# Keys, values and attention output as three float32r passes instead of fp32 products

## The reference

```python
x = x + conv(groupnorm(x))                # 4 experts of 1x1 convolutions, gated per pixel
t = tokens(x)                             # (batch, 784, 96)
t = t + attn(layernorm(t))
t = t + ffn(layernorm(t))                 # weights as signs, activations quantized by groups of 6 images

def attn(x):                              # 12 heads of 8 channels
    q, k, v = split(x @ qkv_w + qkv_b);  q = q * 8 ** -0.5
    fk, fv = f(k), f(v)                   # f(t) = t + 1 if t >= 0 else exp(t)
    A = einsum('bhdn,bhne->bhde', fk, fv) * gauss
    out = einsum('bhnd,bhde->bhne', q, A - lambda_full * A)
    return out @ proj_w + proj_b
```

## Time and profile before

| what | value |
|---|---|
| median of 3 runs | 830.62 us (829.88 to 832.27) |
| span of the profiled execution, first to last instruction | 829.6 us |
| median less span | 1.0 us |
| PE busy | 769.0 us, 93% of the span, 4663 matmul records |
| PE weight loads | 510.4 us, 62% |
| DVE busy | 636.5 us, 77% |
| ACT busy | 476.7 us, 57% |
| POOL busy | 180.2 us, 22% |
| first and last start of a kv product | 93.4 and 651.2 us |

### The profile page before, as it was taken

One profiled execution on the slowest core, in us unless ns is written; L12 is line 12 of the kernel. 1 busy time (PEld: TensorE's weight loads), 2 busy tenths in 40 slices (PEclk: granted clock), 3 DMA queues, 4 the chain that ended last, 5 costly groups with the idle time before them and its releaser, 6 DMA issues.

```text
span 829.6 us, 15136 instructions
## 1 busy us (share of the span) xinstructions
PE 769.0 (93%) x4663; PEld 510.4 (62%) x4663; DVE 636.5 (77%) x1945; ACT 476.7 (57%) x684; POOL 180.2 (22%) x209
## 2 busy tenths in 40 slices
PE   6798899999999999999999999999999999999991
PEld 3465566667666667666666766666766555555540
DVE  3576377877888878788877778887778468999997
ACT  2554445545555554545554555554553499988981
POOL 1440222332223232223232223233222000000000
PEclk8899989999999999999999999999999999999996
DMA  9950011101101101111110101010100101463333
GB/s 217 207 138 16 16 30 30 46 29 29 44 29 29 44 29 29 44 29 29 42 31 29 43 30 29 29 43 29 30 28 15 32 28 53 147 179 113 119 117 116
DMA packets 20351, 48.62 MB, mean 59 GB/s; under 512 B 4937, under 2 KB 5223, under 8 KB 20327
## 3 DMA queue, kind: packets, MB, share of 16 engines
q1 hardware_dynamic: 19928, 47.72, 21.0%
q10 hardware_dynamic: 399, 0.60, 0.3%
HBM read 29.51 MB, written 18.67 MB: 58 GB/s over the span
## 4 chain that ended last, share of the span: by engine, by line
PE 68%; DVE 11%; ACT 8%; issue 7%; SPq 3%; POOL 2%; DMA 1%; ACTq 0%; DVEq 0%; POOLq 0%
PE slot L1010 15%; PE slot L994 9%; PE slot L1017 7%; PE slot L1020 6%; PE slot L1158 6%; PE slot L1055 5%; PE slot L1187 5%; PE slot L1218 4%; PE slot L1222 4%; PE slot L862 4%; DVE stage L1470 4%; ACT stage L759 3%; SPq L442 3%; ACT hT L752 2%; PE slot L926 1%
## 5 line engine op out<-in xcount | busy, mean ns | idle before, releaser
L1436 DVE TENSOR_SCALAR tok<-tok,ln_mv,ln_rs 112x96 f32<-112x96 f32 x434 | 109.2, 322 | 58.2 <-POOL ln_rs L603 58.2
L1010 PE MATMUL slot<-hT,w2s 128*96 128x392 f32 x384 | 135.5, 503 | 3.0 <-ACT hT L752 2.3
L759 ACT ACTIVATE stage<-slot,minus_one 112x768 f32<-112x768 f32 x64 | 52.6, 822 | 125.6 <-PE slot L1055 123.3
L752 ACT ACTIVATE hT<-slot,b1c,w_unit 128x784 f32<-128x784 f32 x96 | 93.1, 1006 | 23.0 <-PE slot L994 23.0
L1010 PEld LDWEIGHTS slot<-hT,w2s 128*96 128x96 f32 x384 | 60.6, 164 | 64.1 <-issue 54.4
L603 POOL TENSOR_TENSOR ln_rs<-ln_ve,pow_half 112x7 f32<-112x7 f32 x62 | 91.8, 1481 | 4.8
L1017 PE MATMUL slot<-big,W1b 99*128 (+1 forms) x360 | 90.3, 332 | 2.1 <-ACT hT L816 0.6
L1020 PE MATMUL slot<-big,W1b 96*128 (+1 forms) x360 | 89.8, 330 | 0.0
L816 ACT ACTIVATE hT<-slot,s 128x784 f32<-128x784 f32 x90 | 80.3, 926 | 6.6 <-DVE stage L1554 6.3
L1442 DVE TENSOR_REDUCE ymax<-slot 128x784 f32 (+1 forms) x90 | 81.1, 956 | 0.1
L600 POOL TENSOR_TENSOR ln_ve<-ln_mv,ln_eps 112x7 f32<-112x7 f32 x62 | 12.5, 202 | 316.2 <-DVE ln_mv L1430 316.2
(11 more groups left out here) (190 smaller groups left out, 1285.2 us busy)
## 6 DMA issues: line engine op xcount, KB each, us to landing
out<-t2T SPq DMA_DIRECT2D x56, 294.0 KB, 2.6
xs<-in_x SPq DMA_DIRECT2D x32, 294.0 KB, 2.8
big<-in_x SPq DMA_DIRECT2D x7, 1176.0 KB, 15.3
xs<-out SPq DMA_DIRECT2D x24, 294.0 KB, 3.3
big<-out SPq DMA_DIRECT2D x1, 1764.0 KB, 11.6
out<-big SPq DMA_DIRECT2D x6, 294.0 KB, 2.6
big<-in_x SPq DMA_DIRECT2D x2, 588.0 KB, 24.1
con<-shape_consts ACTq DMA_DIRECT2D x1, 445.5 KB, 6.3
```

What stands on the lines that cost most here:

```text
L752: nc.scalar.activation(hT[:, t, :].rearrange("p (a n) -> p a n", a=2), halves(t, P), ACT.Relu, scale=w1_unit[:, t:t + 1], bias=b1c[:, t:t ...
L1010: ins = mm(S[k][0:C, h, 0:HALF], w2s[:, v, t, :], hT[:, t, h * HALF:(h + 1) * HALF], start=t == 0, stop=t == TILES - 1, skip_group_check=True)
L1436: ins = V.tensor_scalar(dst[:, j, :], src[:, j, :], ln_mv[n][:, j, 0:1], ln_rs[n][:, j:j + 1], ALU.subtract, ALU.mult)
```

## The change

Keys, values and attention output are each computed in three passes over float32r parts: high x high, high x low, low x high, accumulated in PSUM. The high part is what the former fp32 copy wrote, now with type float32r; the low part is the fp32 value less the high part. ACT writes the high parts xh_hi and R_hi in place of xh1T and R, from the same PSUM and at the same places of its order. DVE gets two new subtractions in each step, each reading PSUM and the high part in SBUF: xh_lo (96x784) between the statistics of tok2 and its normalization, after a wait for the ACT copy, and R_lo (97x96) between the statistics of tok1 and the three maxima, after a wait for the ACT copy of R. PE's kv(0) waits for xh_lo_ready instead of xh1T_ready, and the attention's output for r_lo_ready instead of r_ready. In the setup DVE makes both parts of the weights (two more instructions and two waits on itself), and POOL fills one more row with a constant. Declarations of semaphores and unchanged lines are left out of the diff.

```diff
@@ -168,6 +169,8 @@
         qkvw = sb("qkvw", [C + 1, 3 * C])
+        kvw_hi = sb("kvw_hi", [C + 1, 2 * C], F32R)
+        kvw_lo = sb("kvw_lo", [C + 1, 2 * C], F32R)
...
@@ -248,13 +251,15 @@
-        xh1T = sb("xh1T", [C + 1, HW])
+        xh_hi = sb("xh_hi", [C + 1, HW], F32R)
+        xh_lo = sb("xh_lo", [C + 1, HW], F32R)
...
-        R = sb("R", [C + 1, C])
+        R_hi = sb("R_hi", [C + 1, C], F32R)
+        R_lo = sb("R_lo", [C + 1, C], F32R)
...
@@ -419,7 +427,7 @@
-        CONSTS_SET = (ones_ready, 10)
+        CONSTS_SET = (ones_ready, 11)
@@ -527,8 +535,9 @@
-            pool.wait_ge(ones_ready, CONSTS_SET[1] - 2)
-            nc.gpsimd.memset(xh1T[C:C + 1, :], 1.0).then_inc(ones_ready, 1)
+            pool.wait_ge(ones_ready, CONSTS_SET[1] - 3)
+            nc.gpsimd.memset(xh_hi[C:C + 1, :].bitcast(F32), 1.0).then_inc(ones_ready, 1)
+            nc.gpsimd.memset(xh_lo[C:C + 1, :].bitcast(F32), 0.0).then_inc(ones_ready, 1)
@@ -774,7 +783,7 @@
-                    nc.scalar.copy(*channels(xh1T[0:C, :], 0)).then_inc(xh1T_ready, 1)
+                    nc.scalar.copy(*channels(xh_hi[0:C, :], 0)).then_inc(xh1T_ready, 1)
@@ -792,7 +801,7 @@
-                    nc.scalar.copy(R[:, :], S[3][0:C + 1, 0, 0:C]).then_inc(r_ready, 1)
+                    nc.scalar.copy(R_hi[:, :], S[3][0:C + 1, 0, 0:C]).then_inc(r_ready, 1)
@@ -1034,6 +1043,7 @@
                 pe.wait_ge(projb_loaded, 16)
+                pe.wait_ge(kvw_ready, 1)
@@ -1052,8 +1062,10 @@
                 def kv(q, k, j0, n):
                     for j in range(n):
-                        ins = mm(chunks(k, n, 256, 2 * C)[:, j, :], xh1T[:, (j0 + j) * TOK:(j0 + j + 1) * TOK],
-                                 qkvw[:, C:3 * C], start=True, stop=True, skip_group_check=True)
+                        cols = slice((j0 + j) * TOK, (j0 + j + 1) * TOK)
+                        for p, (x_part, w) in enumerate(((xh_hi, kvw_hi), (xh_hi, kvw_lo), (xh_lo, kvw_hi))):
+                            ins = mm(chunks(k, n, 256, 2 * C)[:, j, :], x_part[:, cols], w[:, :],
+                                     start=p == 0, stop=p == 2, skip_group_check=True)
                     ins.then_inc(kv_ready, 1)
@@ -1119,7 +1131,7 @@
                 if attend:
-                    pe.wait_ge(xh1T_ready, i)
+                    pe.wait_ge(xh_lo_ready, i)
@@ -1182,10 +1194,11 @@
                 if attend:
-                    pe.wait_ge(r_ready, i)
-                    for h in range(2):
-                        ins = mm(S[3][0:C, h, 0:HALF], R[:, :], xh1T[:, h * HALF:(h + 1) * HALF],
-                                 start=True, stop=True, skip_group_check=True)
+                    pe.wait_ge(r_lo_ready, i)
+                    for p, (w, x_part) in enumerate(((R_hi, xh_hi), (R_hi, xh_lo), (R_lo, xh_hi))):
+                        for h in range(2):
+                            ins = mm(S[3][0:C, h, 0:HALF], w[:, :], x_part[:, h * HALF:(h + 1) * HALF],
+                                     start=p == 0, stop=p == 2, skip_group_check=True)
                     ins.then_inc(ao_ready, 1)
@@ -1351,7 +1364,9 @@
-            V.tensor_scalar(qkvw[C:C + 1, C:3 * C], qkvw[C:C + 1, C:3 * C], 1.0, None, ALU.add)
+            link(V.tensor_scalar(qkvw[C:C + 1, C:3 * C], qkvw[C:C + 1, C:3 * C], 1.0, None, ALU.add))
+            link(V.tensor_copy(kvw_hi[:, :], qkvw[:, C:3 * C]))
+            V.tensor_tensor(kvw_lo[:, :], qkvw[:, C:3 * C], kvw_hi[:, :].bitcast(F32), ALU.subtract).then_inc(kvw_ready, 1)
             bn_unit(3, pairs_compared)
@@ -1478,6 +1493,11 @@
                     stats(1, tok2, 2 * i - 1)
+                if attend:
+                    dve.wait_ge(xh1T_ready, i)
+                    V.tensor_tensor(tokenwise(xh_lo[0:C, :]),
+                                    flat(0)[0:C, 0:CHUNKS * P].rearrange("p (j t) -> p j t", t=P)[:, :, 0:TOK],
+                                    tokenwise(xh_hi[0:C, :].bitcast(F32)), ALU.subtract).then_inc(xh_lo_ready, 1)
                 if ffn:
                     apply(1, tok2, tok2, f, xh2_ready)
@@ -1520,6 +1541,10 @@
                     stats(0, tok1, 1 if isinstance(i, int) and i == 0 else 2 * i)
+                if attend:
+                    dve.wait_ge(r_ready, i)
+                    V.tensor_tensor(R_lo[:, :], S[3][0:C + 1, 0, 0:C], R_hi[:, :].bitcast(F32),
+                                    ALU.subtract).then_inc(r_lo_ready, 1)
                 if ffn:
                     for t in range(TILES):
                         absmax(f, t, t)
```

More of the change, by code:

```diff
@@ L13 @@
 BF16 = mybir.dt.bfloat16
+F32R = mybir.dt.float32r
 I32 = mybir.dt.int32
@@ L365, in build @@
         xh1T_ready = sem("xh1T_ready")
+        xh_lo_ready = sem("xh_lo_ready")
+        kvw_ready = sem("kvw_ready")
+        r_lo_ready = sem("r_lo_ready")
         kv_ready = sem("kv_ready")
```

## The result

The changed kernel takes 837.54 us (median of 4 runs, 836.03 to 840.66) beside 831.10 us for the kernel before (4 runs): ratio 1.0079, 95% interval 1.005 to 1.0107. The profiled execution took 837.06 us with a span of 835.3, 5.7 above the span of before.

What follows compares the result with a forecast made beforehand. PE and DVE were taken as co-critical. 29 steps at 0.215 us later give 6.2, the ends 1.4; the sum of 7.6 on the median 830.62 gives 838.2 us, range 820 to 882.

Steps and rivals of the forecast that it cites:

- R_lo's insertion: DVE, ahead of the three maxima: wait for R's copy plus the subtraction insert 0.56 us a step.
- The sum of a step: Steady step, mix to mix: t2 comes 0.25 us later, PE's transposes and mix 0.215 later in the mean.
- kv's gain: kv(0) on PE's path: falls from 1.32 to 1.01 us, so A comes 0.31 earlier.
- Price of a kv pass: PE's keys and values: each pass with its weight load takes 0.084 us, at least 0.081.
- idle time before A: PE before A: the other 0.24 us saved in kv, beyond kv(0)'s 0.31, becomes idle time.
- PE's slack to t2: PE's transposes after DVE's t2: slack 0 in one kind of step and 0.07 us in the other.
- The output: PE's attention output: six passes at 0.166 us, 1.00 against 1.32; starts late for R_lo, ends 0.34 earlier, waits for t2.
- xh_lo hidden: DVE before tok2's normalization: the 0.97 us subtraction lies under POOL's root with 0.3 to spare and costs nothing.
- The ends: Outside the steady loop: +0.7 us in the last step, +0.7 in the first image, setup nothing; 1.4 together.
- PE's busy time: Whole run: PE busy some 20 us less in all, named as a sign that the forecast is right.
- R_lo finds a gap: Rival, DVE from A to t2: room there, so R_lo doesn't delay t2 and the time is 822 us; chance 0.12.
- A pass at half or full price of fp32: Two rivals, PE's passes: half price gives 882 us, chance 0.06; full price 985 or 1050 us, chance 0.14.

Runs made afterwards that it cites:

- output_only: Changed kernel with keys and values as fp32 products over xh_hi alone, attention output still in three passes; 844.57 us, ratio 1.0155.
- r_lo_after_max: Changed kernel with R copied twice by ACT, R_lo made after the first maximum, only the third output pass waiting for it; 828.95 us, ratio 0.9988.
- the last run: Changed kernel with the xh_lo subtraction done twice in the steady loop only, not in the first four images or behind the last mix; 838.19 us, ratio 1.0082.

## Why the prediction was right, and which of its terms were not

The forecast, 838 us as the time and slower as the sign, held; so did its mechanism: A comes earlier, R_lo's insertion on DVE takes more than that, t2 is late, and PE's transposes wait for it. The sum of a step, 0.215, stands against 0.193 measured. But that it came so near is luck: three of its terms were mis-sized, and the errors nearly cancel (kv's gain 0.18 too high, R_lo's insertion 0.14 too high, PE's slack 0.10 too low).

- **Price of a kv pass.** I took 0.084 from the loads of the fp32 transposes; it is 0.099. So kv(0) fell by 0.13 (1.32 to 1.19), not 0.31. The 0.084 came true for float16 parts. The columns that I compared it with were not the limit, as half of them showed. The rule that I weighed (the Trainium skill, "TensorE: Matmul & The Clock Gate", section "LDWEIGHTS (loading the stationary operand)", 93 ns) was nearer for float32r, and above the 84 measured for float16, whose loads have as many columns.
- **R_lo's insertion.** 0.42, not 0.56. R's copy ended 0.092 earlier behind A than before (3.770 to 3.678), which I held fixed; R_lo started 0.03 behind it, not 0.05; and the maxima started 0.20 behind R_lo's start, not 0.253. Wait and instruction are 0.19 + 0.03 + 0.20. R came earlier because kv(1) is on its path, which the prediction denied: of the 0.24 that should have become idle time before A, only 0.09 did (PE's wait there was 0.42 in the mean and is 0.51). PE's transposes behind kv(1) start 0.22 earlier after mix's start, and with them ACT's cast of the feed-forward input, DVE's low part of it (big), PE's first feed-forward tile, which waits for that part in both kernels, and R, while A comes only 0.13 earlier. The low part and the first tile, before and after (A starts at 352.10 and 353.80):

```profile
352.30 0.97 DVE L1514 TENSOR_TENSOR big<-slot,big 96x784 f32 x1 [0.26 <-ACT big L783]
353.56 0.50 PE L1017 MATMUL slot<-big,W1b 99*128 x2
```

```profile
353.91 0.97 DVE L1534 TENSOR_TENSOR big<-slot,big 96x784 f32 x1 [0.17 <-ACT big L792]
355.14 0.50 PE L1026 MATMUL slot<-big,W1b 99*128 x2
```

In output_only, with the fp32 kv, R's copy is back at 3.772 behind A.
- **PE's slack to t2.** I read 0 and 0.07 from two steps, taking the 0.21 between t2's end and the first transpose for signal and load that stay. They don't: while PE waits, the transpose starts 0.06 behind t2. T fell by 0.183, of which the stretch to mix took back 0.05: 0.133 in the mean instead of 0.035.
- **The output.** Six passes at 0.18 (pairs start 0.36 apart at 358.21 and 358.57), not 0.166; PE waits 0.35 for R_lo, not 0.28. Neither counts, as t2 comes later than both.
- **xh_lo hidden.** Right: 0.36 of the wait for POOL is left (0.3 forecast), and a second one was hidden too.
- **The ends.** +0.85 behind the last mix, +0.7 forecast: xh_lo is bare there, between the copy and kv, as the chain shows.

```profile
653.11 0.82 ACT xh_hi L786
653.95 0.98 DVE xh_lo L1498
654.97 2.31 PE slot L1067 x21
```

The setup, costed at nothing, was 1.03 longer in this profile, but the first mix of r_lo_after_max, with the same setup, starts at 73.96; what sets it stays open. In the first image xh_lo was bare as forecast (0.98), but kv(0) took 1.44 instead of 1.57, 0.13 less and not 0.37; and the granted clock in those 1.57 us was 1.00, not a lower one. The first images together, forecast at +0.7, came out at -1.36, which lies within their scatter (below).
- **PE's busy time** fell by 5.9 us, not 20. It counts overlapping records: kv's was 2.51 a step before and 2.52 after (50.15 and 50.45 over 20 steps), since its first record now starts 0.47 ahead of mix's end (349.51 against 349.98). As a check on passes it was a bad sign; their spacing is a good one.

Of the rivals, "R_lo finds a gap" failed as argued: with R_lo behind the first maximum the time was 828.95, with no R_lo at all 825.37. A pass at half or full price of fp32 didn't occur.

## What to carry to other kernels

Where two engines are co-critical, price an inserted instruction by when its operand arrives at that place in the queue: the subtraction for R_lo cost 0.42 us a step ahead of the maxima, where it waited, and 0.17 behind the first of them; one nearly four times as long cost nothing where the engine waits anyway. Splitting an fp32 product pays only by what of it lies on the path (for A four of the seven kv products here, for R all seven; of the output next to nothing), and the pass price comes from the spacing of starts in the same type, not from records or another type's loads. A sum that comes out right can hold three wrong terms: measure the intervals of the step, not only the step.

## What the runs showed of the hardware that I had not expected

Passes of 192 columns with a 112-column load of their own took 0.099 us each in float32r and 0.084 in float16, over the twelve of kv(0); with half the columns in two of three, the float32r loads still started 0.098 apart. Short DVE instructions whose records last 0.25 let the next one start after 0.16 to 0.20. And the start-up varies between executions of the same instructions: the last run has the changed kernel's program in the first four images, but from the second mix to the fourth it took 45.21 us against 42.41. The windows (us, PE busy, granted clock, DMA share, GB/s), first of the changed kernel, then of that run:

```profile
109.00:131.00 22.00, 20.19 (x124) 1.00 0.11 29
...
112.00:115.00 3.00, 2.66 (x19) 1.00 0.00 0
```

```profile
109.00:131.00 22.00, 19.89 (x114) 0.84 0.10 28
...
112.00:115.00 3.00, 1.34 (x7) 1.00 0.00 0
```

A granted clock of 0.84 means that a part of the stretch ran at the lower level (1.2 instead of 2.4 GHz). In that run the granted clock from 118 to 121 us was 0.50; ahead of the fall, from 112 to 115, PE was busy 1.34 us of 3, in the changed kernel 2.66. The changed kernel had 0.50 earlier, from 103 to 106. Which executions keep the clock where wasn't found out, and differences of up to 3 us between single profiles of this kernel should not be read as more than this.
